# First context piece as two transfers, eight fewer idle transposes, and a new order of work on five engines in a cross-attention and feed-forward kernel

## The reference, cut to what matters

```python
# x: 2048 x 256, ctx: 1601 x 256, all float32
q = layernorm(x) @ Wq.T + bq;  k = ctx @ Wk.T + bk;  v = ctx @ Wv.T + bv
s = q @ k.T / 16
s = where(s is among the 32 largest of its row, s, -inf)
x = x + softmax(s) @ v @ Wo.T + bo
# feed-forward with ternary weights and 8-bit activations
bitlinear(x, w, b) = act_quant(rmsnorm(x)) @ weight_quant(w).T + b
x = x + bitlinear(gelu(bitlinear(layernorm(x), w1, b1)), w2, b2)   # 256 -> 1024 -> 256
```

## Time and profile before

| | us |
|---|---|
| median of 3 runs | 285.64 |
| lowest, highest | 285.26, 287.21 |
| the profiled execution, its own time | 285.15 |
| its span in the profile | 283.3 |

### The profile page before, as it was taken

How to read it: one execution, slowest core, us unless ns; L and a number is a source line. 1 busy time by engine, 2 the same in 40 slices (tenths; PEclk the granted TensorE clock), 3 DMA queues, 4 the chain that set the end, 5 groups by cost and what they waited for, 6 DMA issues and landing times. The chain is left out here.

```text
span 283.3 us, 5382 instructions
## 1 busy us (share of the span) xinstructions
PE 263.7 (93%) x1536; PEld 228.6 (81%) x1536; DVE 232.7 (82%) x984; ACT 215.4 (76%) x323; POOL 167.0 (59%) x235
## 2 busy tenths in 40 slices
PE   7999999898997899999999999999999999988784
PEld 7999998897796688787888888878888888867473
DVE  2663778997978897989798979898889997998894
ACT  2657488366599798969797879887988899738762
POOL 3324608921596759676769666975697549712510
PEclk9999999999999999999999999999999999999999
DMA  6981010005000820033002310132003200510011
GB/s 230 312 321 38 3 37 0 22 1 130 1 22 0 168 39 19 2 70 99 19 3 44 108 37 0 27 108 55 0 6 91 56 3 0 130 37 5 0 37 39
DMA packets 29293, 16.44 MB, mean 58 GB/s; under 512 B 20429, under 2 KB 28174, under 8 KB 29262
## 3 DMA queue, kind: packets, MB, share of 16 engines
q1 hardware_dynamic: 28558, 15.02, 19.6%
q0 software_dynamic: 272, 0.79, 1.1%
q10 hardware_dynamic: 432, 0.26, 0.4%
HBM read 9.77 MB, written 2.10 MB: 42 GB/s over the span
## 5 line engine op out<-in xcount | busy, mean ns | idle before, releaser
L398 PE MATMUL bank<-vo,pT 128*128 128x257 f32 (+1 forms) x416 | 97.4, 381 | 3.9 <-ACT pT L1109 3.9
L398 PEld LDWEIGHTS bank<-vo,pT 128*128 128x128 f32 (+1 forms) x416 | 75.9, 190 | 15.2 <-ACT pT L1109 5.4
L1431 DVE MAX8 cand<-s_sb 128x8 f32<-128x50 f32 (+1 forms) x512 | 59.9, 201 | 1.9 <-ACT s_sb L1060 1.1
L257 PE MATMUL score<-k_high,q_low 128*128 128x400 f32 (+1 forms) x128 | 50.2, 393 | 0.0
L871 POOL TENSOR_TENSOR g<-g,b_bc 128x512 f32<-128x512 f32 x24 | 38.7, 1630 | 18.7 <-ACT g L1133 18.7
L257 PE MATMUL score<-k_low,q_high 128*128 128x400 f32 (+1 forms) x128 | 44.2, 346 | 0.0
L257 PE MATMUL score<-k_high,q_high 128*128 128x400 f32 (+1 forms) x128 | 44.0, 344 | 0.0
L1109 ACT ACTIVATE pT<-bank 128x512 f32<-128x512 f32 x64 | 32.0, 517 | 13.3 <-PE bank L265 13.3
L1060 ACT ACTIVATE s_sb<-score 128x400 f32<-128x400 f32 x64 | 31.2, 502 | 8.1 <-PE score L257 8.1
L265 PE MATMUL bank<-ident,e_all 128*128 128x128 f32 (+1 forms) x208 | 31.0, 275 | 5.1 <-DVEq L1505 3.4
L1466 DVE SCALAR_TENSOR_TENSOR e_all<-s_sb,best,e_all 128x1601 f32<-128x1601 f32 x16 | 33.7, 2106 | 1.6 <-ACT e_all L1101 1.2
(11 more groups left out here) (162 smaller groups left out, 492.5 us busy)
## 6 DMA issues: line engine op xcount, KB each, us to landing
x_in<-in_x SPq DMA_DIRECT2D x16, 128.0 KB, 2.3
w_sb<-in_L_ffn_w SPq DMA_DIRECT2D x2, 1024.0 KB, 12.8
x_res<-in_x SPq DMA_DIRECT2D x16, 128.0 KB, 2.2
out<-o_sb SPq DMA_DIRECT2D x16, 128.0 KB, 2.0
ctx_sb<-in_ctx SPq DMA_DIRECT2D x3, 512.0 KB, 6.4
b_bc<-in_L_ffn_b POOLq DMA_DIRECT2D x1, 512.0 KB, 7.6
w_q<-in_L_xattn_Wq SPq DMA_DIRECT2D x1, 256.0 KB, 3.1
w_k<-in_L_xattn_Wk ACTq DMA_DIRECT2D x1, 256.0 KB, 4.3
```

The costliest lines, as they stand in the source:

```text
L257: ins = pe.matmul(out, a, b, start=(i == 0), stop=(i == len(steps) - 1))
L398: ins = pe.matmul(bank[:, 0:DV], pT[0:n, t % 2, b * P:(b + 1) * P], vo[0:n, b, :], start=(b == 0), stop=(b == SB - 1))
L1431: ins = dve.max(cand[:, t % 2, k:CAND:PIECES], s_sb[:, t % 2, k * PIECE:end])
```

## The change

The first 512 KB piece of the context becomes two pieces of 256 KB (blocks 0 and 1, blocks 2 and 3); within a piece a partition holds two neighbouring lines instead of four. `warm` has 22 transposes instead of 30, `hold_clock` 23 instead of 24. Everything else is the order of the calls in the five lists. No helper changes its instructions, apart from which piece `turn_context` waits for. The core of the diff (the tails of ACT, DVE and POOL hold further swaps of neighbours of the same sort: POOL's last two `keep_residual` after `root_2`, ACT's `gelu(13)` ahead of `take_weights(15, 2)`, DVE's `centre(13)` one stretch of candidates later but ahead of `output(9)`):

```diff
-WARM = 30
+CTX_PARTS = ((0, 2), (2, 4), (4, 8), (8, 12))
+WARM = 22
...
@@ TensorE, opening @@
             turn_context(0)
             fold_queries()
             turn_context(1)
+            fold_key_bias()
             turn_context(2)
-            fold_key_bias()
             turn_context(3)
+            project_keys(0, 0)
+            project_keys(0, 1)
             turn_context(4)
-            project_keys(0, 0)
+            project_keys(1, 0)
             turn_context(5)
...
             project_values(1)
-            project_values(2)
+            project_keys(3, 0)
             project_keys(3, 1)
             scores(0, 0)
             scores(0, 1)
             scores(0, 2)
             scores(0, 3)
+            scores(1, 0)
+            project_values(2)
+            scores(1, 1)
             project_values(3)
             project_values(4)
-            scores(1, 0)
+            scores(1, 2)
             project_values(5)
-            scores(1, 1)
 
             for r in range(7):
                 if live(r - 1):
-                    turn_weights(2 * r - 1, 1)
-                    weighted(2 * r - 1, 0)
+                    turn_weights(2 * r - 1, 3)
                 if r == 0:
                     weight_mean()
-                if live(r):
-                    scores(2 * r + 1, 2)
                 if live(r - 1):
-                    turn_weights(2 * r - 1, 2)
+                    weighted(2 * r - 1, 1)
+                    weighted(2 * r - 1, 2)
                 if r == 0:
                     project_values(6)
                 if live(r - 1):
-                    turn_weights(2 * r - 1, 3)
-                    weighted(2 * r - 1, 1)
-                    weighted(2 * r - 1, 2)
                     weighted(2 * r - 1, 3)
+                if live(r):
+                    scores(2 * r + 1, 3)
+                    turn_weights(2 * r, 0)
+                    turn_weights(2 * r, 1)
                 if live(r - 3):
                     down(2 * r - 5)
-                if live(r):
-                    turn_weights(2 * r, 0)
-                    scores(2 * r + 1, 3)
                 if live(r + 1):
                     turn_queries(r + 1)
                 if live(r):
-                    turn_weights(2 * r, 1)
+                    turn_weights(2 * r, 2)
                     weighted(2 * r, 0)
-                    turn_weights(2 * r, 2)
+                    weighted(2 * r, 1)
                     turn_weights(2 * r, 3)
-                    weighted(2 * r, 1)
...
                     scores(2 * r + 3, 0)
                 if live(r):
                     turn_weights(2 * r + 1, 0)
+                    turn_weights(2 * r + 1, 1)
+                if live(r - 2):
+                    down(2 * r - 4)
                 if live(r + 1):
                     scores(2 * r + 3, 1)
-                if live(r - 2):
-                    down(2 * r - 4)
...
+                    scores(2 * r + 3, 2)
+                if live(r):
+                    turn_weights(2 * r + 1, 2)
+                    weighted(2 * r + 1, 0)
...
             turn_weights(14, 2)
             down(10)
             weighted(14, 0)
+            down(11)
+            turn_y1(6)
             weighted(14, 1)
+            up(12, 0)
             turn_weights(14, 3)
-            turn_y1(6)
-            down(11)
-            up(12, 0)
...
+            turn_y1_tile(15)
             turn_y2(13, 1)
-            turn_y1_tile(15)
...
-            hold_clock(24)
+            hold_clock(23)
@@ SyncE @@
-            for k in range((SB - 1) // CTX_PIECE):
-                lo, hi = k * CTX_PIECE, (k + 1) * CTX_PIECE
+            for k, (lo, hi) in enumerate(CTX_PARTS):
...
             turn_counts(5)
+            turn_counts(6)
+            load_x(5)
+            turn_y2(2)
+            store(0)
             load_residual(6)
-            turn_counts(6)
-            turn_y2(2)
-            load_x(5)
-            store(0)
+            load_residual(7)
             store(1)
-            load_residual(7)
             turn_y2(3)
             turn_counts(7)
@@ GpSimd, opening @@
             normalise(1, 1)
             ternary(0, w1_sb)
+            residual(0)
             split_queries(1)
+            residual(1)
+            ternary(1, w2_sb)
             normalise_scale(2)
-            ternary(1, w2_sb)
             normalise(2, 0)
-            residual(1)
-            residual(2)
@@ GpSimd, loop @@
             for r in range(3):
-                if live(r + 1):
-                    keep_residual(r + 1, 1)
-                if live(r + 3):
-                    residual(2 * r + 7)
-                if live(r + 4):
-                    residual(2 * r + 8)
                 if live(r + 2):
-                    keep_residual(r + 2, 0)
+                    add_bias(2 * r + 4, 0)
+                    add_bias(2 * r + 4, 1)
+                    add_bias(2 * r + 5, 0)
+                    add_bias(2 * r + 5, 1)
+                    keep_residual(r + 2, 1)
+                if live(r + 5):
+                    normalise_scale(r + 5)
+                    normalise(r + 5, 0)
+                if live(r + 2):
+                    row_scales_2(r + 2)
                 if live(r + 5):
                     normalise(r + 5, 1)
                 if live(r + 3):
                     row_scales_1(r + 3)
                     quantise_1(r + 3, 0)
                     quantise_1(r + 3, 1)
+                if live(r + 4):
+                    residual(2 * r + 8)
+                if live(r + 3):
+                    keep_residual(r + 3, 0)
                 if live(r + 5):
                     split_queries(r + 5)
-                if live(r + 3):
-                    add_bias(2 * r + 6, 0)
-                    add_bias(2 * r + 6, 1)
-                if live(r + 6):
-                    normalise_scale(r + 6)
...
+                if live(r + 4):
+                    residual(2 * r + 9)
@@ ScalarE, loop @@
                 if live(r):
                     take_weights(2 * r + 1, 2)
+                if live(r + 1):
+                    copy_scores(2 * r + 3, 0)
+                    copy_scores(2 * r + 3, 1)
...
                     take_weights(2 * r + 1, 3)
+                if live(r + 1):
+                    copy_scores(2 * r + 3, 2)
                 if live(r - 1):
                     quantise_2(2 * r - 2)
...
+                    copy_scores(2 * r + 3, 3)
                     take_weights(2 * r + 2, 0)
-                    copy_scores(2 * r + 3, 2)
+                    take_weights(2 * r + 2, 1)
@@ ScalarE, tail @@
             copy_scores(15, 3)
-            take_weights(14, 0)
             quantise_2(11)
             lower_2(11)
+            take_weights(14, 0)
             take_weights(14, 1)
@@ VectorE @@
             count(0)
             weigh(0)
+            largest_count(0)
+            weight_means()
+            release(0)
...
                 if live(r - 1):
-                    attended(2 * r - 1)
                     moments(2 * r - 1)
-                if r == 0:
-                    weight_means()
-                if live(r - 3):
-                    output(2 * r - 5)
-                if live(r - 1):
                     centre(2 * r - 1)
                 if live(r):
                     candidates(2 * r + 1, 0)
+                if live(r - 3):
+                    output(2 * r - 5)
+                if live(r):
                     candidates(2 * r + 1, 1)
                     candidates(2 * r + 1, 2)
                     candidates(2 * r + 1, 3)
-                    best_8(2 * r + 1, 0)
                 if live(r + 2):
                     ln1_stats(r + 2)
                 if live(r):
+                    best_8(2 * r + 1, 0)
```

More of the change, by code:

```diff
@@ L166, in build @@
         wff_in = sem("wff_in")
-        ctx_in = [sem(f"ctx_in_{k}") for k in range(-(-SB // CTX_PIECE))]
+        ctx_in = [sem(f"ctx_in_{k}") for k in range(len(CTX_PARTS) + 1)]
         x_in_done, stored = sem("x_in_done"), [sem(f"stored_{k}") for k in range(4)]
@@ L268, in turn_context @@
             def turn_context(k):
-                pe.wait_ge(ctx_in[2 * k // CTX_PIECE], 16)
+                pe.wait_ge(ctx_in[sum(hi <= 2 * k for _, hi in CTX_PARTS)], 16)
                 blocks = []
@@ L1744, in _ @@
                     weigh(2 * r + 2)
-            largest_count(12)
-            centre(10)
-            release(12)
-            attended(11)
+                    largest_count(2 * r + 2)
+                if live(r):
+                    centre(2 * r)
+                if live(r + 1):
+                    release(2 * r + 2)
+                if live(r):
+                    attended(2 * r + 1)
             moments(11)
-            output(7)
             centre(11)
             candidates(13, 0)
+            output(7)
             candidates(13, 1)
@@ L1767, in _ @@
             release(13)
-            centre(12)
             gelu_max(10)
@@ L1778, in _ @@
             count(14)
+            centre(12)
             weigh(14)
@@ L1783, in _ @@
```

(4 more changed lines are left out.)

288 lines of the change are left out of this document (125 added, 163 removed).

## The result

| | before | after |
|---|---|---|
| median of the runs, us | 285.78 (285.26 to 287.21, 4 runs) | 279.70 (279.27 to 279.85, 4 runs) |
| profiled execution, us | 285.15, span 283.3 | 279.27, span 277.2 |
| up to the release of tile 4 | 95.8 | 93.6 |
| tile 4 to tile 12, four rounds | 116.1, 29.03 a round | 112.9, 28.23 a round |
| tile 12 to the end of the span | 71.4 | 70.7 |

The ratio is 0.9778, 95% interval [0.9758, 0.9797]: faster by 2.2%. Of the 6.1 us that the span lost, 2.2 lie ahead of tile 4, 3.2 in the four middle rounds, and 0.7 behind tile 12.

What follows compares the result with a forecast made beforehand. The round was taken as bound by a loop through DVE and POOL as much as by PE. The terms -1.85 + 0.25 - 0.6 - 0.48 - 0.2 = -2.9 took 285.15 to 282.3 us, range 278.5 to 286.0.

Steps and rivals of the forecast that it cites:

- rival A: Middle rounds: POOL reaches `row_scales_2` late, the even `weigh` begins first (1.88), PE becomes the bound; 278.6 us, chance 0.22.
- What bounds it: Middle rounds: a loop through DVE and POOL as much as PE's; better order wins at most 1.0 us a round.
- Opening, -1.1: Start of PE: eight fewer idle transposes (0.87) and no 0.22 wait for the last large piece, 1.1 us gained.
- First tiles, -1.85: Up to the release of tile 2: earlier `weight_means` and POOL's new order end `ternary(1)` at 51.0, 1.85 us earlier.
- (a): Odd tile, each round: `output` moved behind the first candidates, so `add_bias` starts ahead of `weigh`; `gelu_max` gains 0.4 us.
- (b): Even tile, each round: `normalise` (1.23) replaces `keep_residual` (0.72) just before `weigh`; DVE loses 0.51 us more.
- (c): Even tile, each round: POOL idle beside `centre(2r)`, which takes 0.34 us instead of 0.62; 0.28 back.
- +0.25: First round with a feed-forward part: no `output` to move, so it pays (b) less (c), 0.25 us lost.
- -0.6: Four more rounds at a gain of 0.17 us each: 0.7, of which 0.6 was counted.
- `split_queries` and SyncE's queue at nothing: Middle rounds: later `split_queries` and SP's `load_residual` behind `store` and `turn_y2` lose nothing if no transfer is late.
- Tail, -0.2: End of the kernel: reordered calls partly fill PE's wait for POOL, against ACT's extra 2.4 us; gain 0.2 us.
- The 0.48: Last `up` of the loop: a single gain of 0.48 us, from (a).

## Why the prediction was right, and where it was not

The forecast was 282.3 and the measured median 279.70: inside the range, faster by over 1% as the larger chance had it, but at twice the forecast gain. What came is close to the number of rival A (278.6, a round of 28.2, PE the bound), without A's reason. The time lies in the range because the range was drawn down to A; the mechanism of the forecast did not bring it there, and that is luck.

- *What bounds it.* Right. The round was a loop through DVE and POOL with at most 1.0 to win; 0.80 of it was won and the round went with DVE's even tile one for one (0.45 in the run that put an add back).
- *Opening, -1.1.* The size of the edit was right, the instant of the clock was not. The step that failed is "the clock is no cost: these eight are dropped from the end of the row, after the spacing has already become the fast one". It took the instant of that step, 4.35, from one profile. In the profile after it came at 7.05; the first context transpose came at 6.27 and `fold_queries` at 7.09, 0.44 later than before instead of 1.1 earlier. That is the luck of two executions, not the edit: between profiles with a like step eight transposes fewer bring `fold_queries` 0.9 earlier (last section). In the times no gain is shown, and one of up to 0.9 is not ruled out.
- *First tiles, -1.85.* It hung on the opening. `weight_means` waits for a PE product that came at 40.94 and not, as before, at 39.34: one more quarter of scores stands ahead of it (1.1, as the prediction said), and the opening was 0.44 late where it should have been 1.1 early. So `ternary(1)` was over 0.4 earlier, not 1.85, and `weigh(1)` ended 0.44 earlier. The release of tile 2 came 1.1 earlier (65.56 against 66.70). In the profile in which the step came at 4.57 it came at 64.53, 2.2 earlier, and `ternary(1)` was over at 51.4, where the prediction had 51.0. What brings the release forward beyond `weigh(1)` was not taken apart.
- *(a), 0.4 a round.* Mis-sized. Who goes first is as foretold from tile 7 on: `add_bias` 1.27, `weigh` 2.97. But the second `add_bias` still ends 1.1 behind `weigh`, and `gelu_max` gained 0.2 against the release. The profiles of the old opening in the new order and of the earlier normalise hold both outcomes with otherwise like rounds: 28.3 from release to release where `weigh` goes first (two rounds each), 28.1 to 28.2 where the add does. So the outcome of that pair is worth some 0.15 a round. The move of `output` is worth far more for another reason: it must stand behind, because TensorE's `down` moved too (0.95 a round in the run that put it back).
- *(b), a loss of 0.51.* Wrong sign, and the term that decides. "Whichever starts first goes through" was read off pairs in which GpSimd ran an addition of two tensors, or a pass over 2048 elements. The normalise is another kind of instruction, and it did not hold `weigh` up at a lead of 0.05 or of 0.32. The gain from `weigh` was 0.45 a round: 0.96 away from the term. In all ten profiles in which a normalise stands there `weigh` takes 1.89 to 1.91; why the normalise yields is not shown.
- *(c), 0.28.* Right: 0.62 to 0.33.
- *The sum, stretch by stretch, from release to release.* Up to tile 2: forecast -1.85, measured -1.1. Tile 2 to 4: +0.25 and -0.9. Tile 4 to 12: -0.6 and -3.4. Behind tile 12: -0.68 and -0.6. The whole gap between 2.9 and 6.0 thus lies in the five rounds, where -3.95 is to be explained: 0.96 for (b) in each is 4.8, less some 0.2 a round for (a). Only (b) changes which of the cases comes out. (Among the chances, three fifths of 0.48 and all of 0.22 make 0.51, not 0.52, which changes nothing.)
- *`split_queries` and SyncE's queue at nothing.* Right in effect: no wait of PE for either.
- *Tail, -0.2.* Nearly nothing: from the release of tile 14 to the end 43.2 pass, 43.3 before. PE's wait of 1.72 at 238 is the price of ACT's two extra passes. The price was foreseen, and that it is hidden by the next wait only the two runs showed. The 0.48 that the prediction added once at the last `up` of the loop did come: 27.5 from tile 12 to tile 14 instead of 28.0.
- *The rule of A.* A had POOL late by 0.3 and so `weigh` first. GpSimd was not late: `row_scales_2` starts 21.8 behind the release of the even tile, and 22.0 before, and the normalise began 0.05 ahead of `weigh`. A's size was about right, its mechanism was not.

## What to carry to other kernels

When two engines contend, price the pair that will stand there by a pair of the same two operations: a row of another kind of instruction on the same engine gave the wrong sign here. Orders of several engines belong together: GpSimd's could be moved alone and paid, VectorE's on top of it, without TensorE's, cost 8.7 us (a part of it by the granted clock), and one `output` in its old place cost some 4 us. Before filling a wait, look at what arrives at the next one. And before two openings are compared by one profile each, look at where the clock's step stands in both.

## What the runs showed of the hardware

**Which GpSimd instruction holds `weigh` up.** All beside the same `weigh` (128x1601, 1.88 alone):

| GpSimd instruction | start against `weigh` | its time (alone) | `weigh` |
|---|---|---|---|
| add of two tensors, 128x256 | 0.06 ahead | 0.72 (0.72) | 2.34 |
| add of two tensors, 128x512 | 0.02 behind | 1.27 (1.27) | 2.97 |
| the same, in the run with the earlier normalise | 0.04 behind | 2.97 (1.27) | 1.88 |
| pass over one tensor, 128x2048 | 0.93 ahead | 1.94 (1.94) | 2.69 |
| normalise, one tensor and two columns of scalars | 0.05 ahead | 2.87 (1.23) | 1.89 |
| the same | 0.32 ahead | 1.23 (1.23) | 1.90 |
| power of two tensors, 128x2 (tile 1, in the run with VectorE's order too) | 0.35 ahead | 0.73 (0.73) | 1.88 |

The Trainium skill's rule of an exclusive lock for a whole instruction ("SBUF — State Buffer", section "SBUF: two separate sides") agrees with the first, third and fourth lines. It agrees with the second and the fifth only if the order in which the lock is taken can differ from that of the recorded starts, by 0.02 and by 0.05. It does not agree with the sixth, where both ran for 0.91 at full speed. Nor does it with the last: there GpSimd was still at work 0.38 into `weigh`, and in the lines in which `weigh` loses it ends 1.68 to 1.7 behind GpSimd's instruction, which would have made it 2.06. The measurement decides: a normalise in front of `weigh` costs `weigh` nothing. It is not free for GpSimd, which lost 1.64 in it at a lead of 0.05 and 1.19 in the instruction behind it at 0.32. What in the instruction makes it so (the columns of scalars, its source, its length) was not tried; the last line says that "two tensors" alone is not what holds `weigh` up.

For the add of 128x512 the order turns 0.03 behind the recorded start of `weigh`, and sharply: in the fourteen profiles the add went first wherever it started up to 0.032 behind, and `weigh` wherever the add started 0.033 or more behind. Both occur within one profile, that of the earlier normalise (`weigh` 2.99 at tile 7, 1.88 at tile 11). A pair as close as this is decided by hundredths of a microsecond that no order of calls can place.

**The first step of TensorE's clock.** The idle transposes follow each other at 0.213 (the 1.2 GHz level) and then at 0.109 (2.4 GHz). The windows print a granted clock of 1.00 for the slow part too, as the trace's record of the clock only begins with the step. The engine had started at 1.52 and worked without a break in every profile, and yet the step comes at another instant in each, from 4.35 to 7.60 in fourteen profiles. Six of them:

| profile | idle transposes | step | `fold_queries` | tile 0 released |
|---|---|---|---|---|
| before | 30 | 4.35 | 6.65 | 41.29 |
| the opening alone | 22 | 5.94 | 6.55 | 41.18 |
| the normalise in front, alone | 30 | 7.10 | 7.99 | 42.63 |
| the normalise 0.3 earlier | 22 | 4.57 | 5.88 | 41.65 |
| after | 22 | 7.05 | 7.09 | 42.71 |
| the old opening in the new order | 30 | 5.33 | 7.13 | 42.75 |

With a step near 7.1, 22 transposes instead of 30 bring `fold_queries` 0.90 earlier; with a step near 4.5, 0.77, and another 0.1 if both had stepped at once. That is the prediction's 0.87. The step itself moves `fold_queries` by half of what it moves: 1.34 between the two profiles with 30 whose steps lie 2.75 apart. What `fold_queries` gains or loses, the release of tile 0 passes on: it comes 34.6 behind it in the first three profiles and 35.6 to 35.8 in the last three, where VectorE does `weight_means` first. So one execution's luck is worth as much as the edit. That may be why the edit does not show in the medians; it is not shown.

**The fall near the end.** The profiled execution of the kernel with the earlier normalise took 281.04. TensorE in its last stretch:

```profile
269.90:270.40 0.50, 0.00 (x0) 0.00 (x0) 0.46 (x3) 0.43 (x1) 0.02 (x1) 1.00 0.00 0
270.40:270.90 0.50, 0.06 (x1) 0.06 (x1) 0.50 (x2) 0.50 (x2) 0.00 (x0) 0.91 0.00 0
270.90:271.40 0.50, 0.50 (x3) 0.50 (x4) 0.28 (x1) 0.46 (x1) 0.00 (x0) 0.50 0.00 0
...
273.00:274.00 1.00, 1.00 (x7) 0.72 (x5) 0.61 (x1) 0.00 (x0) 0.00 (x0) 0.50 0.00 0
```

PE waits 1.47 for ACT there, until 270.85, and at the end of the wait the granted clock goes to 0.50, the 1.2 GHz level, for 3.4 us. From the release of tile 12 to the end this execution takes 73.3, where that of after takes 70.7. In two more profiles (`output` ahead, `down(11)` behind `y`) the clock falls in the last 0.2 us of the same wait, and with VectorE's order in the old kernel at the end of a wait of 1.92 in the opening. In the profile of after the same wait of 1.47 passed at 1.00. The fall happens in some executions only: three of four of that kernel, with mean clocks of 0.991 to 0.994, took 280.19 to 281.04, and the one at 1.00 took 279.34. In the run of `output` ahead the five at 0.999 or more took 283.58 to 284.51 and the five at 0.993 took 285.81 to 286.43. With 12 idle transposes in the wait none of six executions fell below a mean of 0.997. Of 59 executions of the kernel before, run beside the experiments, none fell below 0.996, and of the changed kernels only three have no such execution: GpSimd's and SyncE's order alone, one add back, and this one with the twelve. A mean of 0.994 does not always cost time: in the kernel after one such execution took 279.73 and the others 279.27 to 279.85, and with the takes in front two took 279.93 and 280.06 against 279.50 and 279.89. Where the clock fell in those is not shown, as they were not profiled. So a median here moves by up to 2 us with how many executions had the fall, and kernels closer than that are best compared at equal mean clock.
